# Keeping the gate's chosen indices of all batches as integers, and converting them in two operations at the end of the stage

## The reference, cut to what matters

```
gate = einsum('bsd,ed->bse', x, gate_w) + gate_b
_, idx = top_k(gate, 2)
counts = zeros((E,)).at[idx.reshape(-1)].add(1.0)
expert_out = relu(einsum('bsd,ehd->bseh', x, expert_w) + expert_b)
out = einsum('bseh,e->bsh', expert_out, counts) / total
```

## Time and profile before

| what | value |
|---|---|
| time, median of 3 executions | 1035.46 us |
| the three executions | 1033.33, 1035.46, 1038.14 us |
| span of the profiled execution | 1032.2 us |
| TensorE busy | 939.8 us (91%) |
| VectorE busy | 754.4 us (73%) |
| ScalarE busy | 544.4 us (53%) |
| GpSimd busy | 553.0 us (54%) |
| first stage, steady steps | about 65 us to 455 us |
| first stage, drain | about 455 us to 508 us |

### The profile page before, as it was taken

The page is one execution under the profiler, slowest core; times in us unless marked ns, Lnnn a source line. Parts: engine busy times, 40 slices in busy tenths (PEclk is TensorE's granted clock), DMA queues, the critical chain, the costliest instruction groups (busy, mean ns, idle before and its releaser), DMA issues. The chain is left out here.

```text
span 1032.2 us, 31395 instructions
## 1 busy us (share of the span) xinstructions
PE 939.8 (91%) x10664; PEld 663.0 (64%) x10664; DVE 754.4 (73%) x2101; ACT 544.4 (53%) x1068; POOL 553.0 (54%) x897
## 2 busy tenths in 40 slices
PE   4799999999999999998699999999997279999994
PEld 2466666666666666665456666666664169889893
DVE  4678888888888887886677888888875536656673
ACT  3566666666666666666414444444444146555551
POOL 6755555554555455530114777777777634565536
PEclk9999999999999999998799999999998689999998
DMA  5553344344433443423156555565565147786544
GB/s 155 166 155 106 115 134 138 105 118 128 140 108 113 130 139 110 119 85 113 51 150 171 184 183 183 183 183 183 185 187 157 54 123 179 178 191 120 93 78 57
DMA packets 107277, 140.54 MB, mean 136 GB/s; under 512 B 23929, under 2 KB 92592, under 8 KB 106928
## 3 DMA queue, kind: packets, MB, share of 16 engines
q1 hardware_dynamic: 94594, 121.38, 40.0%
q0 software_dynamic: 12528, 17.18, 9.1%
HBM read 93.38 MB, written 38.35 MB: 128 GB/s over the span
## 5 line engine op out<-in xcount | busy, mean ns | idle before, releaser
L997 DVE TENSOR_REDUCE smax<-psum 112x2 f32<-112x750 f32 x240 | 221.5, 935 | 45.3 <-PE psum L449 43.4
L829 ACT ACTIVATE probsT<-psum 125x896 f32<-125x896 f32 x173 | 158.8, 918 | 54.0 <-PE psum L464 52.4
L2022 POOL DMA_INDIRECT out_dram<-y,token_at x63 | 100.4, 1593 | 95.4 <-DVE y L2201 48.0
L1720 DVE SCALAR_TENSOR_TENSOR acc<-psum,neg_bias,acc 128x448 f32<-128x448 f32 x112 | 75.9, 679 | 10.8 <-PE psum L1543 9.3
L484 PE MATMUL psum<-probsT,v_aug 125*32 125x112 f32 x2688 | 81.6, 262 | 0.0
L449 PE MATMUL psum<-k_stack,q_stack 63*128 63x375 f16 x480 | 78.4, 326 | 3.5 <-DVE smax L997 0.7
L1462 POOL DMA_INDIRECT dispatch_dram<-rows,slots_at x64 | 64.0, 1000 | 28.4 <-issue 28.4
L1543 PE MATMUL psum<-xT_hi,we_hi 128*128 128x448 f16 x256 | 70.2, 356 | 1.1 <-ACT we_hi L1642 1.1
L402 POOL CAST k_hi<-we 128x375 f16<-128x375 f32 x64 | 31.9, 498 | 72.5 <-ACT we L849 72.4
L464 PE MATMUL psum<-q_stack,k_stack 64*128 64x112 f16 x1384 | 64.2, 212 | 7.0 <-DMA q_stack<-neg_max 2.3
L1543 PE MATMUL psum<-xT_lo,we_hi 128*128 128x448 f16 x256 | 70.1, 356 | 0.0
(11 more groups left out here) (299 smaller groups left out, 2445.6 us busy)
## 6 DMA issues: line engine op xcount, KB each, us to landing
k_stack<-k_hi_dram SPq DMA_DIRECT2D x64, 188.0 KB, 2.8
we<-in_ctxT_dram SPq DMA_DIRECT2D x32, 375.0 KB, 3.7
ctxT<-in_ctxT_dram SPq DMA_DIRECT2D x32, 375.0 KB
ctx_rows<-in_ctx_dram SPq DMA_DIRECT2D x32, 375.0 KB
w_raw<-in_w_dram SPq DMA_DIRECT2D x32, 256.0 KB, 3.8
rows_e<-dispatch_dram SPq DMA_DIRECT2D x24, 272.0 KB
k_hi_dram<-k_hi SPq DMA_DIRECT2D x32, 188.0 KB, 3.1
k_lo_dram<-k_lo SPq DMA_DIRECT2D x32, 188.0 KB, 3.5
```

Of the source, the lines that this page charges most:

```text
L829: nc.scalar.activation(probsT[:, p, c, hg, :, :, :].rearrange("p k h q -> p k (h q)"), psum[0:KC, 0:2, 0:4 * S], ACT.Exp, scale=float(HD) ...
L997: nc.vector.reduce_max(smax[:, (u - LAG_B) % 2, 2 * (s % 4) + s // 4::PAIRS], psum[0:S, pair_bank(s):pair_bank(s) + 2, 0:KV], AX.X).then_i ...
L1720: nc.vector.scalar_tensor_tensor(out, psum[:, mix_bank(t, u, k), 0:GT], neg_bias[:, hc, e:e + 1], out, ALU.max, ALU.add).then_inc(m["acc_r ...
L2022: nc.gpsimd.indirect_dma_start(dram["out"], bass.IndirectOffsetOnAxis(token_at[:, unit // PAIR % TOKEN_TURNS, unit % PAIR:unit % PAIR + 1] ...
```

## The change

The eight indices that VectorE finds for a batch used to go to one small tile (`top8_at`, 8 integers), and the first two of them were converted at once into the batch's place in `chosen_at` (float). Now `top8_at` has room for all 32 batches (32 x 8 integers a partition), the index operation writes its batch's place in it, and the conversion is gone from the steps and from `choice`. A new function `chosen_of(first, last)` converts a range of batches in one operation that reads two of every eight integers: in the drain once for batches 0 to 29, ahead of `marks(0, B - 2)`, and once for batches 30 and 31, ahead of the last `marks`. The semaphore `choice_ready` is raised two times a batch instead of three.

```
-    top8_at = sb("top8_at", [S, 8], U32)
+    top8_at = sb("top8_at", [S, B, 8], U32)
...
                 if e:
-                    wait(dve, m["choice_ready"], count(t, u - LAG_E, 3, 1))
+                    wait(dve, m["choice_ready"], count(t, u - LAG_E, 2, 1))
                     apart(dve)
-                    nc.vector.max_index(top8_at[:], top8[:], logits[:]).then_inc(m["choice_ready"], 1)
+                    nc.vector.max_index(top8_at[:, be, :], top8[:], logits[:]).then_inc(m["choice_ready"], 1)
                 pair_max(2)
-                if e:
-                    wait(dve, m["choice_ready"], count(t, u - LAG_E, 3, 2))
-                    nc.vector.tensor_copy(chosen_at[:, bass.ds(be * 2, 2)], top8_at[:, 0:2]).then_inc(m["choice_ready"], 1)
                 if d:
...
             def choice(b):
...
-                dve.wait_ge(m["choice_ready"], 3 * b + 2)
-                nc.vector.tensor_copy(chosen_at[:, 2 * b:2 * b + 2], top8_at[:, 0:2]).then_inc(m["choice_ready"], 1)
+            def chosen_of(first, last):
+
+                dve.wait_ge(m["choice_ready"], 2 * last)
+                nc.vector.tensor_copy(chosen_at[:, 2 * first:2 * last].rearrange("p (b n) -> p b n", n=2), top8_at[:, first:last, 0:2]).then_inc(m["counted"], 1)
...
             norm_rows(last)
-            dve.wait_ge(m["choice_ready"], 3 * (B - 2))
+            chosen_of(0, B - 2)
+            dve.wait_ge(m["counted"], 1)
             marks(0, B - 2)
...
             choice(last)
-            dve.wait_ge(m["choice_ready"], 3 * B)
+            chosen_of(B - 2, B)
+            dve.wait_ge(m["counted"], 5)
             marks(B - 2, B, gate_counts[:, 1:5, :])
```

More of the change, by code:

```diff
@@ L1061, in step @@
                     wait(dve, m["gate_done"], count(t, u - LAG_E, 1, 1))
-                    wait(dve, m["choice_ready"], count(t, u - LAG_E - 1, 3, 3))
+                    wait(dve, m["choice_ready"], count(t, u - LAG_E - 1, 2, 2))
                     nc.vector.tensor_tensor(logits[:], psum[0:S, 5, 0:E], gate_bias[:], ALU.add).then_inc(m["logits_ready"], 1)
@@ L1146, in choice @@
                 dve.wait_ge(m["gate_done"], b + 1)
-                dve.wait_ge(m["choice_ready"], 3 * b)
+                dve.wait_ge(m["choice_ready"], 2 * b)
                 nc.vector.tensor_tensor(logits[:], small[0:S, GATE_AT:GATE_AT + E], gate_bias[:], ALU.add).then_inc(m["logits_ready"], 1)
@@ L1150, in choice @@
                 nc.vector.max(top8[:], logits[:]).then_inc(m["choice_ready"], 1)
-                dve.wait_ge(m["choice_ready"], 3 * b + 1)
-                nc.vector.max_index(top8_at[:], top8[:], logits[:]).then_inc(m["choice_ready"], 1)
-                dve.wait_ge(m["choice_ready"], 3 * b + 2)
-                nc.vector.tensor_copy(chosen_at[:, 2 * b:2 * b + 2], top8_at[:, 0:2]).then_inc(m["choice_ready"], 1)
+                dve.wait_ge(m["choice_ready"], 2 * b + 1)
+                nc.vector.max_index(top8_at[:, b, :], top8[:], logits[:]).then_inc(m["choice_ready"], 1)
+            def chosen_of(first, last):
+                dve.wait_ge(m["choice_ready"], 2 * last)
+                nc.vector.tensor_copy(chosen_at[:, 2 * first:2 * last].rearrange("p (b n) -> p b n", n=2), top8_at[:, first:last, 0:2]).then_inc(m["counted"], 1)
             def heads_scaled(b):
@@ L1230, in _ @@
             norm_rows(last)
-            dve.wait_ge(m["choice_ready"], 3 * (B - 2))
+            chosen_of(0, B - 2)
+            dve.wait_ge(m["counted"], 1)
             marks(0, B - 2)
             norm_low(last)
-            dve.wait_ge(m["counted"], 1)
+            dve.wait_ge(m["counted"], 2)
             nc.vector.tensor_reduce(most_counts[:], is_chosen[:, 0:2 * (B - 2), :].rearrange("p n e -> p e n"), AX.X, ALU.add).then_inc(m["counted"], 1)
-            dve.wait_ge(m["counted"], 2)
+            dve.wait_ge(m["counted"], 3)
             nc.vector.tensor_copy(gate_counts[:, 0, :], most_counts[:]).then_inc(m["counted"], 1)
             choice(last)
-            dve.wait_ge(m["choice_ready"], 3 * B)
+            chosen_of(B - 2, B)
+            dve.wait_ge(m["counted"], 5)
             marks(B - 2, B, gate_counts[:, 1:5, :])
```

## The result

The changed kernel takes 1021.08 us (median of 6 executions, 1016.68 to 1023.00), the kernel before beside it 1034.45 us (6 executions, 1032.15 to 1038.14). The ratio is 0.9847, with a 95% interval of 0.9825 to 0.9869: 1.5% faster, 15.8 us by the ratio and 13.4 by the medians. The forecast was 12.7 us.

The account below looks back on a forecast made before the run. TensorE sets the step, held up by VectorE from the third maximum to `onT_lo`. Steps 12.5 + drain 0.2 = 12.7 us less, so 1035.5 - 12.7 = 1022.8 us; range 1019.5 to 1028.5.

Parts of the forecast that it names:

- The stall and its cause: In the steady steps, VectorE's two-index conversion takes 0.72 us because it waits for GpSimd's `k_lo`.
- The rule of the Trainium skill: Casts can use a two-port mode sharing a port pair with GpSimd; whoever comes second blocks fully: 0.72 us against 0.17.
- estimate of 4.2 us: By a fixed term of about 150 cycles, a conversion would be 0.16 us, 27 of them at most 4.2 us.
- What reached TensorE, 12.5 us: Steady steps, second to fourth block of transposed scores: 24 steps give 0.50 us each, two give 0.24 and 0.3, one nothing.
- The drain, 0.2 us: Four of the drain's five batches lose a conversion of about 0.17 us; gain 0.2 us, ends 0 and 0.7.
- The wait passes to the next operation: The reciprocal, now inside `k_lo`, is blocked instead; gain under 2 us, 1033.5 to 1035.5; 5 in 100.
- The transfer takes part back: Negated maxima arrive late in a third of the steps, 6 us lost, about 1028.8 us; 12 in 100.
- It takes back more than all: Late negated maxima cost over 0.47 us every step, making the kernel slower, at worst 1047 us; 3 in 100.
- The clock in the drain: TensorE's mean clock there, 0.83, may shift: a few us either way; 6 in 100 for a time below 1019.5.

Follow-up runs that it names:

- changed, conversion back: Changed kernel with a two-index conversion put back at its old place in every gate step, into a tile nothing reads: 1036.60 us, ratio 0.9992.
- by a reduction: Kernel before with the in-step conversion made by a maximum over an axis of length one, at the same place: 1023.70 us, ratio 0.9855.
- conversion later: Kernel before with the in-step conversion and its wait moved behind `o_nat`: 1023.97 us, ratio 0.9862.
- k_lo in two parts: Kernel before with each GpSimd `k_lo` made by two operations, of 128 and 247 columns: 1024.64 us, ratio 0.9886.
- cover taken away: Changed kernel with the drain's wide conversion and the marks of 30 batches moved behind `xT_lo` of the last batch: 1024.26 us, one execution.
- transposition early: Changed kernel with TensorE's transposition of the maxima put between the first two value blocks: 1029.59 us, ratio 0.9929.

## Why the prediction was right in its mechanism, and where its size was off

**The stall and its cause.** Right. That the conversion's 0.72 us was a wait for GpSimd was read from one end time and three other lengths; three experiments now show it from three sides (another operation, another time, a shorter GpSimd operation).

**The rule of the Trainium skill.** The traces agree with the page "SBUF — State Buffer", section "Who interferes with whom": the reduction, which the page counts among the operations that never contend on trn2, took 0.14 us inside `k_lo`, and the reciprocal, with its input in PSUM, its usual 0.25. The estimate of 4.2 us from the fixed term of the Trainium skill's page "VectorE: DVE Perf Modes" was a good price for the operation (27 unblocked conversions measured 4.3 us) and a bad one for the kernel, which regained three times as much.

**What reached TensorE, 12.5 us.** Right. The stages of all profiled executions, in us, each the difference between two starts in a trace: A from the first instruction to the second block of transposed scores of step 4, B from there to that of step 31, C from there to the first product of the mixture, D the rest of the span.

```
                               A        B        C        D      span
kernel before                57.12   397.15    55.84   522.09   1032.2
kernel before, again         56.17   397.23    57.40   522.60   1033.4
changed, conversion back     58.37   397.30    56.89   521.74   1034.3
changed kernel               57.92   384.98    55.30   520.50   1018.7
changed kernel, again        56.34   385.15    56.14   523.87   1021.5
by a reduction               58.40   385.67    55.26   524.27   1023.6
conversion later             58.42   385.93    54.97   522.98   1022.3
k_lo in two parts            57.20   385.72    54.41   522.67   1020.0
cover taken away             57.05   385.52    56.45   522.98   1022.0
transposition early          57.35   391.73    54.95   520.68   1024.7
```

B holds the lengths of 27 steps, 26 of them with a conversion; it is the same within 0.2 us in the three executions with the stall, and 12.2 us shorter in the two executions of the changed kernel (385.07 on average against 397.23). The 0.50 of the last step falls into C. Together 12.7 us, where the forecast had 12.5.

That it is so close is partly luck, since two errors cancel. The step at 263 us was counted as giving 0.50, for its conversion of 0.72, and gives 0.23: its distance was 3.88 before. There an exponential of ScalarE starts 0.27 us late, though nothing that the profile shows held it (a gap of 0.16 us put down to "issue"), and with it the second block, while VectorE was on time. Every trace has this at the same place, and in the changed kernel it makes a step of 14.48 us:

```profile
256.91 0.92 ACT L829 ACTIVATE probsT<-psum 125x896 f32<-125x896 f32 x1 [0.16 <-issue]
```

Against it the transfer of the negated maxima made three steps of the steady part longer by 1.05 us together before and by 0.8 in the changed kernel, which the forecast did not count: 0.3 us of gain.

**The drain, 0.2 us.** C is 0.9 us shorter in the changed kernel than in the kernel before (55.72 against 56.62 on average), 0.5 of which is the last step's. That would leave 0.4 for the drain, within the ends of 0 and 0.7, but the two values of the kernel before differ by 1.6. And C does not follow the drain's program. The conversion put back has the new drain and 56.89; the three kernels with the old drain and no stall have 54.41 to 55.26. So the drain's own 0.2 us is neither shown nor ruled out. What C goes with is TensorE's mean clock (the changed kernel's row, the clock third from the end):

```profile
442.90:498.20 55.30, 42.29 (x737) 29.21 (x738) 36.29 (x90) 29.01 (x46) 7.11 (x16) 0.88 0.22 67
```

Its third value from the end is 0.88. Over the same stage it is 0.85 in all three executions with the stall (C of 55.84 to 57.40), 0.87 or 0.88 in the kernels with a reduction, a later conversion, `k_lo` in two parts and the early transposition (54.41 to 55.26), and 0.86 with the cover taken away and in the second execution of the changed kernel (56.45 and 56.14). TensorE's busy time in C, for the same matmuls, is 43.6 to 43.8 us at 0.85 and 42.2 to 42.7 at 0.87 or 0.88. The same kernel shows both 0.88 and 0.86, so this is in part an execution's chance; whether steps without the stall also bring it about was not tried.

**Where the size was off.** The sum forecast 12.7 us, the ratio says 15.8 (13.5 to 18.1). 1034.45 x 0.9847 = 1018.6 us lies below the range's end of 1019.5, though the median of the executions, 1021.08, lies inside. The step that failed is the last one, from the sum to the range: "with 6 in 100 for a time below 1019.5". I had put the lower end at the profiled span less the sum, and so left the scatter of an execution out on that side, although the three times shown were 4.8 us apart and the range reached 5.7 us up. D, which the change does not touch, goes from 520.50 to 524.27 in the table; the first profile of the changed kernel has the shortest. The five runs without the stall and without other costs (the changed kernel is two of them) have ratios of 0.9847, 0.9862, 0.9855, 0.9862 and 0.9886 (the last with 0.03 us more in a step), on average 0.9862 or 14.3 us, and all their intervals but the first's hold 12.7. The estimate itself moves with the way it is made: the plain means of the changed kernel and of the kernel before are 14.1 us apart in the first comparison (1020.5 against 1034.7) and 13.1 in the second (1023.3 against 1036.5), and the two profiled spans of each are 12.7 apart on average (1020.1 against 1032.8). The traces place 12.7 in the steps. For all the rest the forecast had 0.2 us, and there the traces differ by some us from one execution of a kernel to the next (C by 1.6 in the kernel before, D by 3.4 in the changed one). Whether the other 1 to 2 us are a second effect, the clock in C, or the scatter of the last stages stays open: executions without a profile can't be split into stages.

**The rivals.** *The wait passes to the next operation*: did not happen, the reciprocal took 0.25 us. *The transfer takes part back*: the mechanism is there and smaller than priced. In the trace of the changed kernel three steady steps are longer than 14.21 by 0.45, 0.11 and 0.22 us because of it, 0.8 us together; there are 2.0 us of waits as before, in four places instead of three, the fourth behind the last steady step. Before, three steps were longer by 0.27, 0.21 and 0.57, and 0.96 of these 1.05 us came back, since the conversion then met less of `k_lo`; now the 0.8 are lost in full. *It takes back more than all*: nothing of it. *The clock in the drain*: 1 to 1.6 us of TensorE's busy time between the executions, as told above; the forecast had "a few us to either side".

**What remains: the same kind of stall elsewhere.** The fifth long step, 14.56 us in both executions of the changed kernel, comes once, at about 140 us; in the other kernels, but for the early transposition, the same step is 0.35 to 0.38 us longer than its neighbours too (14.62 with `k_lo` in two parts, 15.06 to 15.08 with the stall). It starts with `x1n`, the normalized residual that VectorE makes and TensorE transposes (GpSimd, VectorE, TensorE; first that step, then the next):

```profile
136.13 0.52 POOL L418 TENSOR_SCALAR mask_all<-mask_all 32x375 f32<-32x375 f32 x1
136.19 1.32 DVE L1123 TENSOR_SCALAR x1n<-x_res,ln_mv,ln_rstd 112x256 f32<-112x256 f32 x1
136.62 0.72 POOL L388 TENSOR_TENSOR x_res<-x_res,bo 112x256 f32<-112x256 f32 x1
137.56 0.20 PEld L560 LDWEIGHTS psum<-ident,x1n 112*128 112x128 f32 x2 [0.17 <-DVE x1n L1123]
...
150.71 0.73 POOL L388 TENSOR_TENSOR x_res<-x_res,bo 112x256 f32<-112x256 f32 x1
150.77 0.82 DVE L1123 TENSOR_SCALAR x1n<-x_res,ln_mv,ln_rstd 112x256 f32<-112x256 f32 x1
```

In the drain, where no operation of GpSimd runs beside it, an `x1n` takes 0.41 us. In every other steady step it takes 0.81 or 0.82, starts 0.06 or 0.07 us into GpSimd's `x_res` and ends 0.15 behind it: by its times it is held as the conversion was. It costs nothing there, because TensorE comes to it only at 151.96, 0.37 us after its end. At 136 us it outlasted two of GpSimd's operations, 1.32 us, and TensorE waited. No run changed this, so that GpSimd holds `x1n` is read from the times alone.

## What to carry to other kernels

A tiny operation on VectorE that takes several times its length while GpSimd is busy is a wait, and the end times show it: compare both engines' ends before pricing its removal, and look in the same trace for steps where it fell outside. There are then four cures, here all worth about the same: leave it out, move it by 0.7 us, use an operation of a kind that isn't held up, or cut GpSimd's operation. The last was tried on the conversion alone, and `x1n`, which outlasted two operations in a row, says that it need not work for every operation. What such a stall costs is read on the engine that sets the step, as the distance between two of its own instructions around the place, best in a step that happens to lack the stall: 0.56 us of waiting were worth 0.50 here, and the floor showed that nothing more was to be had. `x1n`, by its times, is held for 0.4 us in every step, and in all but one it costs nothing.

## What was not expected

- Cutting GpSimd's `k_lo` of 375 columns (0.90 us) in two costs little: 128 columns take 0.43 us and the second part starts 0.38 us after the first and takes 0.66 for 247, so 1.04 us in all, and the kernel is 11.8 us faster by its ratio.
- A single transposition of TensorE put between two blocks of value products makes a step 0.29 us longer, some nine times what the late transfers cost that it was meant to cure (0.29 x 26 = 7.5 us a run against 0.8).
- Converting 60 integers that lie 2 of 8 apart takes 0.18 us, against 0.17 for two.
